# First group of a decoder layer: odd score steps in idle PSUM banks, low parts on GpSimd, and matrix products that nobody reads in the waits behind the scores

## The reference, cut to what matters

```python
x = layernorm(x + attn(x))          # linear attention, 16 heads of 16; q and k are products of two projections
x = layernorm(x + xattn(x, ctx))    # long convolution of pairwise channel products, filter of 128 taps
x = layernorm(x + ffn(x))           # 256 -> 2048 (gate, up, gelu) -> 256, weights in 4 bits with block scales

# in attn, per head, before the output projection:
s = causal_mask(q @ k.T); o = s @ v
o = o * rsqrt(mean(o * o) + eps) * norm_w

# in ffn, once for all tokens:
W = LUT4[codes] * scales            # gate, up and down
```

## Time and profile before

| | us |
|---|---|
| median of 3 runs | 580.69 (579.39 to 581.28) |
| the profiled execution | 580.05 |
| its span | 578.4 |
| PE busy | 524.9 (91%) |
| VectorE busy | 375.6 (65%) |
| ACT busy | 148.2 (26%) |
| POOL busy | 123.5 (21%) |

### The profile page before, as it was taken

How to read it: one execution, slowest core, us unless ns; L and a number is a source line. 1 busy time by engine, 2 the same in 40 slices (tenths; PEclk the granted TensorE clock), 3 DMA queues, 4 the chain that set the end, 5 groups by cost and what they waited for, 6 DMA issues and landing times.

```text
span 578.4 us, 9097 instructions
## 1 busy us (share of the span) xinstructions
PE 524.9 (91%) x3280; PEld 428.4 (74%) x3280; DVE 375.6 (65%) x782; ACT 148.2 (26%) x259; POOL 123.5 (21%) x195
## 2 busy tenths in 40 slices
PE   5855569989989999999999999999999998599993
PEld 5722457776778888876788888776888887488883
DVE  3899659976768566886355577875455768733234
ACT  3422210153243211242232112232232110122220
POOL 2100038420001445030002445120003443200001
PEclk9965569999999999999999999999999999699998
DMA  5523214130020111005000110031001110100001
GB/s 164 160 79 73 71 53 132 56 95 16 21 72 23 43 37 47 0 29 156 1 1 28 47 47 28 0 88 57 0 0 44 47 54 1 37 1 0 1 1 37
DMA packets 25249, 26.69 MB, mean 46 GB/s; under 512 B 2816, under 2 KB 22784, under 8 KB 25216
## 3 DMA queue, kind: packets, MB, share of 16 engines
q1 hardware_dynamic: 14208, 15.73, 9.4%
q10 hardware_dynamic: 10576, 8.95, 5.2%
q0 software_dynamic: 432, 1.57, 0.8%
HBM read 24.15 MB, written 2.10 MB: 45 GB/s over the span
## 4 chain that ended last, share of the span: by engine, by line
PE 81%; DVE 11%; issue 3%; DMA 3%; POOL 1%; ACT 1%; ACTq 0%; POOLq 0%; DVEq 0%; SPq 0%
PE bank L903 16%; PE bank L905 15%; PE bank L904 15%; PE front_bank L1015 5%; PE front_bank L1018 4%; PE front_bank L1016 4%; PE front_bank L964 4%; PE front_bank L951 4%; PE front_bank L992 3%; PE front_bank L903 2%; PE front_bank L904 2%; PE front_bank L905 2%; DVE gate_q L676 2%; PE front_bank L974 1%; DMA wo_sb<-in_woT 1%
## 5 line engine op out<-in xcount | busy, mean ns | idle before, releaser
L903 PE MATMUL bank<-x2T_lo,ffn_hi 128*128 128x512 f32 x256 | 111.1, 434 | 4.1 <-DVE x2T_lo L838 4.1
L854 DVE TENSOR_TENSOR inter<-bank,inter 128x512 f32<-128x512 f32 x64 | 44.2, 690 | 94.3 <-PE bank L905 94.0
L905 PE MATMUL bank<-x2T_hi,ffn_hi 128*128 128x512 f32 x256 | 101.8, 397 | 0.0
L904 PE MATMUL bank<-x2T_hi,ffn_lo 128*128 128x512 f32 x256 | 101.4, 396 | 0.0
L436 POOL TENSOR_TENSOR qbd<-qT_sb,ctxT_sb 128x256 f32<-128x256 f32 x128 | 77.8, 631 | 77.5 <-PE front_bank L1018 63.8
L386 POOL TENSOR_TENSOR ve<-ve,minus_half 128x2 f32<-128x2 f32 x24 | 17.4, 743 | 305.5 <-DVE ve L726 235.4
L903 PE MATMUL bank<-ffn_lo,inter_hi 128*128 128x256 f32 x256 | 77.2, 302 | 0.8 <-DVE inter_lo L848 0.8
L588 ACT ACTIVATE inter_hi<-inter 128x512 fp32r<-128x512 f32 x64 | 40.5, 632 | 141.9 <-DVE inter L854 141.9
L582 ACT ACTIVATE inter<-bank 128x512 f32<-128x512 f32 x64 | 38.2, 598 | 134.3 <-PE bank L905 134.2
L905 PE MATMUL bank<-ffn_hi,inter_hi 128*128 128x256 f32 x256 | 72.0, 281 | 0.0
L904 PE MATMUL bank<-ffn_hi,inter_lo 128*128 128x256 f32 x256 | 71.9, 281 | 0.0
(11 more groups left out here) (113 smaller groups left out, 768.9 us busy)
## 6 DMA issues: line engine op xcount, KB each, us to landing
toep_sb<-in_toep ACTq DMA_DIRECT2D x64, 128.0 KB, 2.1
xT_sb<-in_xT SPq DMA_DIRECT2D x4, 512.0 KB, 6.1
ctxT_sb<-in_ctxT SPq DMA_DIRECT2D x4, 512.0 KB, 4.7
x_sb<-in_x SPq DMA_DIRECT2D x4, 512.0 KB, 5.7
ctx_sb<-in_ctx SPq DMA_DIRECT2D x4, 512.0 KB, 6.8
out<-ctxT_sb POOLq DMA_DIRECT2D x3, 512.0 KB, 3.4
raw_w<-in_gate_p SPq DMA_DIRECT2D x8, 128.0 KB
raw_s<-in_gate_s SPq DMA_DIRECT2D x8, 128.0 KB
```

The lines of the kernel that those rows point to most:

```text
L854: nc.vector.tensor_tensor(inter[:, n % 2, :], up_ps[:, :], inter[:, n % 2, :], ALU.mult).then_inc(inter_ready, 1)
L903: nc.tensor.matmul(ps, w_hi, x_lo, start=start, stop=False, skip_group_check=True)
L904: nc.tensor.matmul(ps, w_lo, x_hi, start=False, stop=False, skip_group_check=True)
L905: return nc.tensor.matmul(ps, w_hi, x_hi, start=False, stop=stop, skip_group_check=True)
```

## The change

Four things, all but one for group 0 alone:

- **Odd score steps elsewhere.** For group 0, raw scores of odd steps go to the four feed-forward banks (now one tensor, `ffn_ps`), and their masked scores to `odd_sc_sb`, a view of `inter`. PE's order in group 0 becomes raw scores(u), values(u-1), and raw scores(u) wait for mask(u-2). Mask(u) waits for values(u-1) if u is even, for values(u-2) if it is odd.
- **Low parts on GpSimd.** The subtraction of L645 leaves VectorE's piece; GpSimd makes it one piece earlier (unit n-1 in piece n), in all pieces, also in those beside group 1's front.
- **Products that nobody reads.** `keep_busy` issues 4 single passes of 128x512 behind the last score step, 15 behind the head sums, 8 behind the factor transposes, 10 behind the output projection and 4 behind the transposes of x1, for group 0. They write `down_ps[1]` and wait for nothing.
- In GpSimd's turn, the first low part stands ahead of `spread(g, 1)` and the others behind it.

```diff
+        odd_sc_sb = inter[:].rearrange("p n (h c) -> p (n h) c", c=P)
-        psum = [None] * 4 + [stack.enter_context(nc.psum_tensor(f"bank{i}", [P, T], F32)) for i in range(4, 8)]
+        ffn_ps = stack.enter_context(nc.psum_tensor("ffn_bank", [P, 4, T], F32))
...
+        def alone(g):
+            return isinstance(g, int) and g == 0
+        def scores_ps(g, u):
+            return ffn_ps if alone(g) and u % 2 else front_ps
+        def masked_scores(g, u):
+            return odd_sc_sb if alone(g) and u % 2 else sc_sb
...
@@ gpsimd
+            def unpack(step):
+                n = step - 1
+                if 0 <= n < NU:
+                    m, c = units[n]
+                    pool.wait_ge(whi_ready, n + 1)
+                    nc.gpsimd.tensor_tensor(ffn_lo[:, m, :, c * QC:(c + 1) * QC], weight[:, n % 2],
+                                            ffn_hi[:, m, :, c * QC:(c + 1) * QC].bitcast(F32), ALU.subtract)\
+                        .then_inc(wlo_ready, 1)
...
                 if g is not None:
-                    for pair in range(4):
+                    beside(0)
+                    spread(g, 1)
+                    for pair in range(1, 4):
                         beside(pair)
-                    spread(g, 1)
...
@@ vector, unpack
-                q = n - 2
-                if 0 <= q < NU:
-                    m, c = units[q]
-                    dve.wait_ge(whi_ready, q + 1)
-                    nc.vector.tensor_tensor(ffn_lo[:, m, :, c * QC:(c + 1) * QC], weight[:, q % 2],
-                                            ffn_hi[:, m, :, c * QC:(c + 1) * QC].bitcast(F32), ALU.subtract)\
-                        .then_inc(wlo_ready, 1)
@@ vector, score
-                count(dve, o_mm, NU_S, g, u)
+                count(dve, o_mm, NU_S, g, u - u % 2 if alone(g) else u)
...
@@ tensor
+            def keep_busy(g, times):
+                if isinstance(g, int) and g == 0:
+                    for _ in range(times):
+                        nc.tensor.matmul(down_ps[1], fold_hi[:, 0, 0, 0:P], xT_hi[:, 0, :],
+                                         start=True, stop=True, skip_group_check=True)
...
+            def raw_scores(g, u):
...
+                if alone(g) and u >= 2:
+                    count(pe, sm_ready, NU_S, g, u - 1)
...
             def score(g, u):
+                if alone(g):
+                    if u < NU_S:
+                        raw_scores(g, u)
+                    if u:
+                        values(g, u - 1)
+                    if u == NU_S:
+                        keep_busy(g, 4)
...
@@ behind sums(KT - 1), factor, outproj(1), x1T
+                    keep_busy(g, 15)
+                keep_busy(g, 8)
+                    keep_busy(g, 10)
+                keep_busy(g, 4)
```

More of the change, by code:

```diff
@@ L449, in turn @@
                     pool.dma_start(out_v[:, bass.ds(at, NB), :], res_sb).then_inc(stored, 16)
-            schedule(pool, turn, {"score": score, "norm": norm, "x1T": x1T, "conv": conv}, nothing, nothing, nothing, nothing,
+            schedule(pool, turn, {"score": score, "norm": norm, "x1T": x1T, "conv": conv}, nothing, nothing, nothing, unpack,
                      lambda: rstd(G - 1, 2))
@@ L938, in vproj @@
                 last.then_inc(v_mm, 1)
-            def score(g, u):
-                if u:
-                    v = u - 1
-                    mt, b = v // NB, v % NB
-                    if v == 0:
-                        count(pe, v_ready, 2, g, 2)
-                    count(pe, sm_ready, NU_S, g, v + 1)
-                    for odd in range(2):
-                        for pair in range(4):
-                            last = nc.tensor.matmul(
-                                front_ps[32 * pair:32 * pair + 32, b, 256 + mt * S:256 + (mt + 1) * S],
-                                v_sb[:, b, 4 * mt + pair, DK * odd:DK * odd + 2 * DK],
-                                sc_sb[:, 2 * pair + odd, :], start=odd == 0, stop=odd == 1)
-                    last.then_inc(o_mm, 1)
-                if u < NU_S:
-                    mt, b = u // NB, u % NB
-                    if u == 0:
-                        count(pe, qk_ready, 4, g, 4)
-                        count(pe, v_ready, 2, g, 2)
-                    count(pe, spread_ready[u % 2], NU_S // 2, g, u // 2 + 1)
-                    for r in range(4):
-                        rows = slice(32 * r, 32 * r + 32)
-                        last = nc.tensor.matmul(front_ps[:, r, 0:2 * P].rearrange("p (k c) -> p k c", c=P),
-                                                kT_sb[rows, mt, b * S:(b + 1) * S], q_two[rows, u % 4, 0:2],
-                                                start=True, stop=True)
-                    last.then_inc(s_mm, 1)
@@ new lines, in values @@
+            def values(g, v):
+                mt, b = v // NB, v % NB
+                if v == 0:
+                    count(pe, v_ready, 2, g, 2)
+                count(pe, sm_ready, NU_S, g, v + 1)
+                for odd in range(2):
+                    for pair in range(4):
+                        last = nc.tensor.matmul(
+                            front_ps[32 * pair:32 * pair + 32, b, 256 + mt * S:256 + (mt + 1) * S],
+                            v_sb[:, b, 4 * mt + pair, DK * odd:DK * odd + 2 * DK],
+                            masked_scores(g, v)[:, 2 * pair + odd, :], start=odd == 0, stop=odd == 1)
+                last.then_inc(o_mm, 1)
@@ new lines, in raw_scores @@
+            def raw_scores(g, u):
+                mt, b = u // NB, u % NB
+                if u == 0:
+                    count(pe, qk_ready, 4, g, 4)
+                    count(pe, v_ready, 2, g, 2)
+                if alone(g) and u >= 2:
+                    count(pe, sm_ready, NU_S, g, u - 1)
+                count(pe, spread_ready[u % 2], NU_S // 2, g, u // 2 + 1)
+                for r in range(4):
+                    rows = slice(32 * r, 32 * r + 32)
+                    last = nc.tensor.matmul(scores_ps(g, u)[:, r, 0:2 * P].rearrange("p (k c) -> p k c", c=P),
+                                            kT_sb[rows, mt, b * S:(b + 1) * S], q_two[rows, u % 4, 0:2],
+                                            start=True, stop=True)
+                last.then_inc(s_mm, 1)
@@ L969, in sums @@
+            def score(g, u):
+                if alone(g):
[5 more added lines that the diff above has]
+                        keep_busy(g, 4)
+                else:
+                    if u:
+                        values(g, u - 1)
+                    if u < NU_S:
+                        raw_scores(g, u)
             def sums(g, mt):
```

28 lines of the change are left out of this document (15 added, 13 removed).

## The result

| | before | after |
|---|---|---|
| median, us | 580.03 (579.39 to 581.28) | 583.51 (581.16 to 584.92) |
| the profiled execution, us | 580.05 | 583.91 |
| its span, us | 578.4 | 582.3 |
| VectorE busy | 375.6 | 379.9 |
| POOL busy | 123.5 | 153.8 |

The ratio is 1.0055, with a 95% interval of 1.0039 to 1.0071: the change makes the kernel **slower by 0.55%**, about 3.5 us. I had predicted 578.0 with a range of 571.0 to 583.0.

A forecast was written before the change was run, and what follows sets the result against it. Group 0's front was taken as bound by a chain between engines, VectorE and PE nearly equal. Terms 1.3 + 1.7 + 0.5 - 0.8 - 3.15 - 2.2 + 0 = -2.65 gave 578.0 us on the median, range 571.0 to 583.0.

The forecast's parts named there:

- Score steps: Group 0, mask 1 to mask 7: shifts wait for GpSimd's low parts, 22.9 us against 21.56, +1.3.
- ahead of mask 1: Group 0's unpacking pieces before the first mask: five now each meet a low part, +1.7 us at mask 1.
- four products: Between last mask and head sums: products take 1.72 us at the lower clock against a 1.2 wait, +0.5.
- rival 1: VectorE unpacking: only bit mask and scaling wait for GpSimd, not the shifts; 572.6 us, chance 0.20.
- Sums: Group 0's head sums on PE: the clock was expected to rise inside them, -0.8 us (0 to -1.8).
- Sums to the last residual add: Group 0, through the output projection: last residual add 12.3 us behind the sums instead of 15.46, -3.15.
- To the fifth convolution: Group 0, x1 transposes through first convolutions: faster passes, earlier filter issue, -2.2 us (0 to -3.5).
- Later pieces: Turn to group 1 and slot 6: subtractions leave VectorE, return as waits for GpSimd, 0 us (-1.8 to +1.0).
- Rival 3: Group 0 behind the scores: clock stays low, products delay the output projection to 11.8 behind the sums; 583.4 us, chance 0.08.

The follow-up runs named there:

- e9: e7 plus four-pass products on constants in the last group's turn (7 and 1.5), none in the first group; 574.35 us, ratio 0.9901 to the kernel before.
- e7: Kernel before plus odd banks, low parts of units 4 to 10 on GpSimd held until the causal mask, group 0's spreads on ScalarE, no products; 577.14 us.
- e6: Changed kernel with the low parts of units 15 to 23 back on VectorE, GpSimd keeping units 0 to 14; 581.57 us, ratio 1.0016 to the kernel before.
- e1: Changed kernel with all low parts subtracted by VectorE again, odd banks and products kept; 578.39 us, ratio 0.9958 to the kernel before.
- e12: e9 plus 110 narrow single passes and 2.5 four-pass products in the first group's front, moving the loop's instructions; 573.60 us, ratio 0.9887 to the kernel before.

## Why the prediction was wrong

**Score steps, ahead of mask 1, four products.** Right. I counted 22.9 us from mask 1 to mask 7, measured 22.6, with two long steps of 4.04 and four of 3.62 where I had 4.15 and 3.65; +1.7 at mask 1, measured +1.5; +0.5, measured +0.6 (from mask 7 to the sums). The shifts do wait for GpSimd, so rival 1 is out. They had no row in the trace before, and I placed them by their slope. By the Trainium skill (SBUF — State Buffer, Who interferes with whom) the causal mask, which has one input in SBUF, should not wait; the trace agrees (1.22 beside a low part in e9), and that is what e7 builds on.

**Sums.** Wrong by 0.65. The clock was to rise inside them; it rose at about 67.7 us, in the fifteen products. This also made these longer than the wait, 5.24 instead of 3.45, but the projection waited for VectorE all the same. I had also read the clock's fall in the earlier trace rows as 2.4 us after PE stopped; 3.2 us at a mean of 0.93 are a fall after 2.7.

**Sums to the last residual add.** Right: 12.5 behind the sums, I had 12.3.

**To the fifth convolution.** Wrong by about 1.1. "Transposes of x1 are paced by the normalisation and save 0.4" leaves out that a low part stands beside the normalisation; that instruction has two operands for each partition and waits as well. Behind the last residual add, the first convolution starts 0.8 later than before, where I had 0.4 earlier. The fifth starts at 90.21 against 91.38, so 1.2 earlier, where the sum had 2.65.

**Later pieces.** This is the step that failed: "They leave VectorE and come back as waits for GpSimd: 0 (-1.8 to +1.0)". These pieces measured +2.8, which e6 takes back: 0.6 in the turn, 0.6 for the wait in slot 6, and 1.5 for the clock that falls behind it. I had treated the clock as a matter of group 0 only, though PE waits longer in slot 6 and loses it there. The whole part from group 0's skip products to the end measured +5.1. The other 2.3 had no term in my sum: 1.26 are the stall, since I put nothing down for 88 more instructions ahead of a loop, and 1.3 the last turn, which no part of the change is shown to cause.

**The direction.** Without the low parts on GpSimd, the change would have been faster (e1, 0.9958), and with odd banks, low parts and products put where they fit, it is worth 1.1% (e12, which also has products in the last turn). The rivals that I gave had no case in which the loss comes behind group 0. Rival 3 names 583.4, nearly the measured 583.51, but that is luck: it needed fifteen and eight products at the lower level and a projection that starts 11.8 behind the sums, and the projection started 8.7 behind them and took 3.72. My range up to 583.0 left even that rival's number out.

What stays open: why the clock falls at waits of 2.14 and 2.18 and not at one of 1.53 is not settled by these runs, nor is why the kernel before loses less at the end than every other kernel without products there. Whether the 0.8 us between the sum of the parts (+2.7) and the whole (+3.5) are more than noise is open too.

## What to carry to other kernels

Work given to GpSimd isn't gone from VectorE's time by that alone: here it was hidden where it lay beside the causal mask, which reads PSUM, and cost time beside shifts, bit masks, scalings and the normalisation. Put a wait in front of it that sets its place. Look for such pieces in every stage that the change touches, not only in the one that it is meant for. Before products are put into a wait, compare their length at the lower clock with the wait, and hold the clock through every later wait, too. When instructions are added ahead of a loop, count the instruction queue's packets in its later passes: in this kernel a shift by twelve instructions cost 1.3 to 1.7 us, and shifting on to the next packet gave it back.

## What the runs showed of the hardware

In all fourteen kernels the loop of 1736 TensorE instructions was read once where its body touches 7 packets of 256, and again in its second pass where it touches 8 (one boundary lies between instruction 4317 and 4329 as counted here; e12, with its position chosen ahead, fits a next one 256 further on). What in the chip makes 8 too many is not shown. The Trainium skill (Runtime: NRT & Kernel Launch, Instruction fetch mechanics) gives TensorE 128 KiB of instruction memory in blocks of 16 KiB, calls the crossing of a block mostly hidden, and warns that a taken branch stalls for a fetch if its target isn't in the current window of two pages. The packets of 16.4 KB agree, and so does a stall at the jump back, 1.26 to 1.71 us in eight kernels. The window of two pages doesn't: in the six others the jump back spans the same 1736 instructions without a new packet or a stall.

A filter's DMA of 128 KB was on the chain for 4.22 and 4.79 us when issued at 86 us, and for 5.23 to 6.68 when issued at 79 to 85; the traces show the loads of the next group and of the weights in the same stretch, but no run takes them apart.
